# A second layer rewritten: step width first, tanh gate on half differences, fewer activation tables, fills on POOL

## The reference

```python
u = einsum('bld,hd->blh', x, W_x) + b_x                  # 256 hidden channels
g = sigmoid(einsum('bld,hd->blh', x, W_g) + b_g)
h = conv1d(u, conv_w, three taps, one filter per channel) + conv_b
u = u * g + h * (1.0 - g)
dt = clip(softplus(einsum('bld,hd->blh', x, W_dt) + b_dt).mean(axis=(0, 1)), 0.001, 2.0)
A_d = exp(-softplus(A_raw) * dt[:, None])                # 16 states per channel
B_d = (A_d - 1.0) / (A + 1e-06) * B_ssm
new = A_d * carry + B_d * u_t;  y_t = einsum('bhs,hs->bh', new, C_ssm)
attn = layernorm(x + y @ W_out.T + b_out)

gates = softmax(x @ gate_w);  top 2 of 8 experts, weight = sum of both gates
ffn = sum over chosen experts of weight * (gelu(x @ w1_e + b1_e) @ w2_e + b2_e)
```

## Time and profile before

| what | value |
| --- | --- |
| median of 3 runs | 433.61 us (428.1 to 437.87) |
| the profiled execution | 432.72 us |
| its span, first to last instruction | 430.9 us |
| mean granted TensorE clock | 0.951 |
| busy in the span: PE, DVE, ACT, POOL | 373.1, 305.1, 286.6, 168.6 us |

### The profile page before, as it was taken

How to read it: one execution, slowest core, us unless ns; L and a number is a source line. 1 busy time by engine, 2 the same in 40 slices (tenths; PEclk the granted TensorE clock), 3 DMA queues, 4 the chain that set the end, 5 groups by cost and what they waited for, 6 DMA issues and landing times. The chain is left out here.

```text
span 430.9 us, 10083 instructions
## 1 busy us (share of the span) xinstructions
PE 373.1 (87%) x3136; PEld 258.3 (60%) x3136; DVE 305.1 (71%) x1067; ACT 286.6 (67%) x689; POOL 168.6 (39%) x269
## 2 busy tenths in 40 slices
PE   1999999997999999999977999969788659788993
PEld 0444344366887777777764777766242435666982
DVE  4766709654988898989945588766989795384195
ACT  5787768564776776777736566556699942995634
POOL 1403909203787888888868022332000020000013
PEclk9999999999999999999999799989799678898997
DMA  8330323262222222222246100000000010000003
GB/s 227 65 87 12 100 79 105 70 177 68 56 72 70 72 73 73 75 73 73 85 125 152 20 2 2 0 2 0 2 0 1 0 27 2 0 2 0 2 0 99
DMA packets 33148, 23.14 MB, mean 54 GB/s; under 512 B 10062, under 2 KB 32860, under 8 KB 33116
## 3 DMA queue, kind: packets, MB, share of 16 engines
q1 hardware_dynamic: 31868, 22.67, 19.3%
q10 hardware_dynamic: 1248, 0.07, 0.2%
HBM read 13.26 MB, written 9.47 MB: 53 GB/s over the span
## 5 line engine op out<-in xcount | busy, mean ns | idle before, releaser
L486 PE MATMUL psum<-w,hT 128*128 128x385 f32 x128 | 45.5, 496 | 0.7 <-ACT stage L613 0.4
L900 PE MATMUL psum<-win,wst 128*32 128x128 f32 x1024 | 37.4, 277 | 1.3 <-ACT kd L975 1.3
L486 PEld LDWEIGHTS psum<-w,hT 128*128 128x128 f32 x128 | 23.2, 189 | 25.2 <-issue 11.4
L995 ACT ACTIVATE win<-psum 128x512 f32<-128x512 f32 x62 | 32.9, 581 | 0.1
L1266 ACT ACTIVATE std_<-mv_,cst 128x2 f32<-128x2 f32 (+1 forms) x46 | 13.5, 296 | 28.0 <-DVE mv_ L1244 16.4
L900 PEld LDWEIGHTS psum<-win,wst 128*32 128x32 f32 x1024 | 28.3, 109 | 5.5 <-ACT kd L975 1.5
L1004 ACT ACTIVATE bstd<-bmv,cst 128x1 f32<-128x1 f32 x32 | 9.4, 295 | 32.7 <-DVE bmv L1106 32.7
L1494 POOL TENSOR_TENSOR win<-win,lng 128x512 f32<-128x512 f32 x2 | 2.5, 1268 | 71.2 <-ACT win L1779 71.2
L1052 POOL TENSOR_SCALAR xh<-raw,bmv,brs 128x128 f32<-128x128 f32 x32 | 25.4, 793 | 2.7 <-DVE brs L1110 2.6
L1512 PE MATMUL psum<-xn1T,w1e 128*128 128x512 f32 x32 | 18.8, 714 | 7.7 <-ACT he L1673 6.1
L1045 POOL TENSOR_TENSOR xkm<-win,wst 128x256 f32<-128x256 f32 x32 | 19.6, 613 | 14.6 <-PE psum L918 8.4
(11 more groups left out here) (309 smaller groups left out, 1151.5 us busy)
## 6 DMA issues: line engine op xcount, KB each, us to landing
rows_scratch<-stage SPq DMA_DIRECT2D x32, 192.5 KB
win<-rows_scratch SPq DMA_DIRECT2D x32, 192.5 KB, 2.4
attn_scratch<-ob SPq DMA_DIRECT2D x32, 64.0 KB
att<-attn_scratch SPq DMA_DIRECT2D x4, 512.0 KB, 4.1
xt<-in_L_attn_x SPq DMA_DIRECT2D x4, 256.0 KB, 4.1
out<-win SPq DMA_DIRECT2D x4, 256.0 KB, 2.5
cst<-in_constants SPq DMA_DIRECT2D x1, 408.0 KB, 5.1
w<-in_L_attn_wk SPq DMA_DIRECT2D x2, 128.0 KB, 4.3
```

The source lines that it names most:

```text
L486: mm = nc.tensor.matmul(rows_bank(i, h)[:, 0:RC], hT[:, k, i * P:(i + 1) * P], w4[:, k, h, :], start=(k == 0), stop=(k == 1))
L900: mm = nc.tensor.matmul(dst[32 * b:32 * b + 32, 0:F], v[:, at:at + 2 * K], w_sb[:, state, first_slot(b) + h, :], start=False, stop=(h == 1 ...
L995: nc.scalar.activation(own, psum[:, 2 * half:2 * half + 2, 0:H * F].rearrange("p b (h g) -> p b h g", h=H), ACT.Copy).then_inc(w_done, 1)
```

## The change

- The step width's sum is split: softplus(x) = (|x| + x)/2 + ln(1 + exp(-|x|)). The sum of x needs no tile: the copies of the normalized input (`xn1T`) at the end of layer 0 sum up their columns (`accum_out` into `xsum`), and two 16-column products with W_dt follow the logits. Relu goes; Abs sums instead. Exp runs in two halves.
- The gate is 1 - g = (1 + tanh(-z/2))/2. The convolution's weights are halved and u is taken out of its middle tap once (`halve`), so that `conv` gives (h - u)/2, `blend` multiplies it by (gate + 1), and POOL adds u. `conv` writes in place in `uT`, on DVE alone; u has eight buffers.
- PE takes the dt products first and the gate products late, one with each expert tile; `pick` does one tile at a time.
- `decay()` runs after the third blend. ACT loads six tables in the block, not eleven.
- POOL clears `wtap` in four pieces, early, and copies `d0` and half of `wtap`, which ACT did.

```diff
+                m1.halve(nc, pool)
...
-                            ins = nc.scalar.activation(xn1T[:, i * P:(i + 1) * P], bank[6 + p][:, 0:P], ACT.Copy)
+                            ins = nc.scalar.activation(xn1T[:, i * P:(i + 1) * P], bank[6 + p][:, 0:P], ACT.Copy,
+                                                       accum_out=m1.xsum[:, i:i + 1])
                         ins.then_inc(cp_done, 1)
...
+        nc.gpsimd.tensor_scalar(self.cw[:, :, 1], self.cw[:, :, 1], 1.0, None, ALU.subtract).then_inc(self.halved, 1)
+        pool.wait_ge(self.halved, 1)
+        nc.gpsimd.tensor_scalar(self.cw[:], self.cw[:], 0.5, None, ALU.mult).then_inc(self.halved, 1)
+        nc.gpsimd.tensor_scalar(self.cb[:], self.cb[:], 0.5, None, ALU.mult).then_inc(self.halved, 1)
+        nc.gpsimd.tensor_scalar(self.bg[:], self.bg[:], -0.5, None, ALU.mult).then_inc(self.halved, 1)
...
-        gate = region1[:, :].rearrange("p (n l) -> p n l", n=NU)
+        gate = sb("gate", [P, RING, L], c=c)
...
+        region2 = sb("region2", [P, NG * P], c=c)
+        wtap = region2[:, :].rearrange("p (j c) -> p j c", j=NG)
+        gt = region2[:, 0:NT * P].rearrange("p (i q e) -> p i q e", i=NT, q=4)
+        ub = sb("ub", [P, NU, L + 2], c=c)
...
+        ab = region4[:, :].rearrange("p (n l) -> p n l", n=NU)
...
+        pick_bank = lambda n: bank[6 + n % 2]
...
+                def pick(n):
+                    t, q = divmod(n, 4)
+                    two = slice(32 * q, 32 * q + 2)
                     pe.wait_ge(gT_done, 4)
+                    if n >= 2:
+                        pe.wait_ge(gated, n - 1)
+                    nc.tensor.matmul(pick_bank(n)[:, :], con("pick")[two, :], gT[two, t * 512:t * 512 + 512],
+                                     start=True, stop=True).then_inc(pick_mm, 1)
...
+                dt_product(0)
+                for i in range(NT):
+                    nc.tensor.matmul(bank[7][:, i * NE:(i + 1) * NE], xn1T[:, i * P:(i + 1) * P], m1.gate_w[:], start=True, stop=True)
+                for k in range(2):
+                    mm = nc.tensor.matmul(bank[7][:, NT * (NE + k):NT * (NE + k + 1)], wT[:, 2, half(k)], m1.xsum[:], start=True, stop=True)
+                mm.then_inc(gate_mm, 1)
+                dt_product(1)
+                u_product(0)
+                dt_product(2)
+                dt_product(3)
+                for n in range(1, 5):
+                    u_product(n)
+                    dt_product(3 + n)
+                u_product(5)
+                gate_product(0)
+                gate_product(1)
+                pe.wait_ge(gates_done, 1)
+                turn_gates(0)
+                turn_gates(1)
+                u_product(6)
+                u_product(7)
+                up(0, 0)
+                up(0, 1)
+                for i in (2, 3):
+                    pe.wait_ge(gT_done, i - 1)
+                    turn_gates(i)
...
+                    pick(n)
+                    if n + 2 < NU:
+                        up(*divmod(n + 2, 4))
+                        gate_product(n + 2)
                     if n == 5:
+                        down(0)
+                for q in range(4):
+                    up(2, q)
+                    pick(8 + q)
+                    if q == 1:
+                        down(1)
...
+                    nc.scalar.activation(ub[:, n, 1:L + 1], bank[n % 2][:, :], ACT.Identity,
+                                         bias=m1.bx[:, n % 2:n % 2 + 1]).then_inc(u_done, 1)
+                def gate_tile(n):
+                    act.wait_ge(g_mm, n + 1)
+                    if n >= RING:
+                        act.wait_ge(blend_done, n - RING + 1)
+                    nc.scalar.activation(gate[:, n % RING, :], bank[2 + n % 2][:, :], ACT.Tanh,
+                                         bias=m1.bg[:, n % 2:n % 2 + 1], scale=-0.5).then_inc(gate_done, 1)
+                def magnitude(n):
+                    b, k = divmod(n, 2)
+                    act.wait_ge(dt_mm, n + 1)
+                    nc.scalar.activation(ab[:, n, :], bank[4 + n % 2][:, :], ACT.Abs, bias=m1.bd[:, k:k + 1],
+                                         accum_out=dta[:, k, b:b + 1]).then_inc(abs_done, 1)
+                def decayed(i):
+                    act.wait_ge(abs_done, NU // 2 * (i + 1))
+                    tiles = slice(NU // 2 * i, NU // 2 * (i + 1))
+                    nc.scalar.activation(ab[:, tiles, :], ab[:, tiles, :], ACT.Exp, scale=-1.0).then_inc(exp_done, 1)
...
+                act.wait_ge(a_stage, 1)
+                nc.scalar.activation(asp[:], asp[:], ACT.Exp, scale=-1.0).then_inc(a_stage, 1)
+                act.wait_ge(pads, 2)
+                magnitude(0)
+                magnitude(1)
                 u_tile(0)
+                act.wait_ge(mx_done, 1)
+                nc.scalar.activation(ex, lg, ACT.Exp).then_inc(ex_done, 1)
+                magnitude(2)
+                magnitude(3)
                 u_tile(1)
...
+                decayed(0)
+                for n in range(2, 6):
+                    magnitude(2 + n)
+                    u_tile(n)
+                decayed(1)
...
+                u_tile(6)
+                u_tile(7)
...
+                act.wait_ge(gates_done, 1)
+                for n in range(NU):
+                    hidden(*divmod(n, 4))
+                    gate_tile(n)
...
+                act.wait_ge(lnac_done, 1)
+                nc.scalar.activation(a32[:], lnac[:], ACT.Exp, scale=float(TC)).then_inc(a32_done, 1)
...
+                act.wait_ge(ex2_stage, 1)
+                nc.scalar.activation(ex2[:], ex2[:], ACT.Exp).then_inc(ex2_stage, 1)
...
-                nc.scalar.activation(d0[:, :, :, 1:NCH], a32[:, :, None, None].broadcast_to([P, NG, B, NCH - 1]), ACT.Copy).then_inc(d0_done, 1)
+                for q in range(4):
+                    hidden(2, q)
...
+                act.wait_ge(pool_stage, 5)
+                for q in range(2):
+                    nc.scalar.activation(wtap[quad(q), :, quad(q)], x2[quad(q), :, :].rearrange("p c j -> p j c"),
+                                         ACT.Copy).then_inc(taps, 1)
...
+                    b, k = divmod(n, 2)
+                    dst = uT[:, k, row(b)]
+                    dve.wait_ge(u_done, n + 1)
+                    nc.vector.tensor_scalar(dst, ub[:, n, 0:L], cw[:, k, 0:1], cb[:, k:k + 1], ALU.mult, ALU.add).then_inc(conv_done, 1)
+                    for tap in (1, 2):
+                        dve.wait_ge(conv_done, 3 * n + tap)
+                        nc.vector.scalar_tensor_tensor(out=dst, in0=ub[:, n, tap:L + tap], scalar=cw[:, k, tap:tap + 1],
+                                                       in1=dst, op0=ALU.mult, op1=ALU.add).then_inc(conv_done, 1)
...
+                    dve.wait_ge(conv_done, 3 * n + 3)
                     dve.wait_ge(gate_done, n + 1)
-                    nc.vector.tensor_tensor(df[:, p, :], df[:, p, :], gate[:, n, :], ALU.mult).then_inc(diff_done, 1)
-                    dve.wait_ge(diff_done, 2 * n + 2)
+                    nc.vector.scalar_tensor_tensor(out=dst, in0=gate[:, n % RING, :], scalar=1.0, in1=dst,
+                                                   op0=ALU.add, op1=ALU.mult).then_inc(blend_done, 1)
...
+                def decay():
+                    dve.wait_ge(abs_done, NU)
+                    w(nc.vector.tensor_reduce(dts[:], dta[:], AX, ALU.add))
+                    w(nc.vector.tensor_tensor(dts[:], dts[:], dtw[:], ALU.add))
+                    dve.wait_ge(a_stage, 3)
+                    w(nc.vector.scalar_tensor_tensor(out=asp[:], in0=asp[:], scalar=-1.0, in1=bsp[:], op0=ALU.mult, op1=ALU.subtract))
+                    dve.wait_ge(ln_done, 2)
+                    w(nc.vector.scalar_tensor_tensor(out=dt[:], in0=dts[:], scalar=0.5, in1=dtl[:], op0=ALU.mult, op1=ALU.add))
+                    w(nc.vector.tensor_scalar(dt[:], dt[:], 1.0 / TOK, 0.001, ALU.mult, ALU.max))
+                    w(nc.vector.tensor_scalar(dt[:], dt[:], 2.0, None, ALU.min))
+                    nc.vector.tensor_tensor(lna[:], asp[:], dt[:, :, None].broadcast_to([P, 2, NS]), ALU.mult).then_inc(lna_done, 1)
+                    dve.wait_ge(lna_done, 1)
+                    nc.vector.transpose(lnac[:], lna[:].rearrange("p k s -> p (k s)")).then_inc(lnac_done, 1)
+                    for k in range(2):
+                        nc.vector.tensor_tensor(kex[:, k, :, :], lna[:, k, None, :].broadcast_to([P, TC, NS]),
+                                                con("ramp0")[:, :, None].broadcast_to([P, TC, NS]), ALU.mult).then_inc(kex_stage, 1)
+                    dve.wait_ge(lnac_done, 1)
+                    nc.vector.tensor_tensor(ex2[:], lnac[:, :, None].broadcast_to([P, NG, TC]),
+                                            con("ramp1")[:, None, :].broadcast_to([P, NG, TC]), ALU.mult).then_inc(ex2_stage, 1)
+                    w(nc.vector.tensor_scalar(asp[:], asp[:], 1e-6, None, ALU.add))
...
+                gate_logits()
...
```

(37 more changed lines are left out.)

229 lines of the change are left out of this document (41 added, 188 removed).

## The result

The changed kernel takes a median of 442.66 us (439.06 to 443.83, four runs); the kernel before, beside it on the same chip, 432.47 (428.1 to 437.87). The ratio is 1.0222, with an interval of 1.0162 to 1.0281: about two per cent slower, where the forecast was 430.5 and no measurable change. The profiled execution of the changed kernel took 439.06 (span 437.3, mean granted clock 0.941), 6.3 above that of before.

The account below looks back on a forecast made before the run. The second layer's block was taken as a chain passing between engines, none full, with d0 the last wait before the first scan. -5.5 + 1.0 + 1.5 = -3.0 us gave 429.7, or 430.5 on the median's scale; range 424.5 to 439.

Parts of the forecast that it names:

- the step of 3.2: Among the blends before the transposes: one step charged 3.2 us because down(0) stands on PE ahead of pick(6).
- Blends (C): Blend steps from 325.0 to 349.6 us, 24.6 together, with DVE charged 0.92 or 0.65 per POOL add.
- The three steps of 1.9: Among the blends, after the third step that carries decay(): three steps charged 1.9 us each.
- the forecast's 1.0: Behind the scans: the last two picks wait for apply_gate(12) and (13), chunk_out behind them; 0.5 to 1.3, taken as 1.0 late.
- the first rival: POOL's adds don't hold DVE: blend steps lose about 0.65 to 1.0 each, time 425 (421 to 426); chance 0.20.
- d0 was the last wait: Before the first scan: ACT's fill of d0, to 378.49, is the last wait; taking it off ACT is worth 2.0 us.
- the second rival: POOL's copies of d0 and wtap run at the add's rate: 436, or 441 to 443 with transposes held; chance 0.19.
- The third rival: PE at the lower clock level through 325 to 350, among the blends: about 10 us more, 440; chance 0.09.
- the running sums: Ahead of the block: sixteen copies of xn1T each get a running sum; 0.8 to 3.2 us, taken as 1.5.
- B: Convolution, before the first blend: five convs 9.8 us, four gate-row copies 2.6, DVE waiting 3.8 for PE; ends at 325.0.

Follow-up runs that it names:

- e9: The changed kernel with picks 2 to 5 not made, their tiles multiplied by what earlier picks left; median 436.56 us, ratio 1.0074 to before.
- e2: The changed kernel without POOL's eight adds of u to the blended tiles; median 437.4 us, ratio 1.0120 to before.
- e7: The changed kernel with apply_gate(12) and (13) behind the sixth and seventh scan instead of the eighth; median 439.81 us, ratio 1.0060 to before.
- e3: The changed kernel with down(0) behind pick(7) on PE and add_experts(0) between the two transposes on DVE; median 437.47 us, ratio 1.0138 to before.
- e1: The changed kernel with picks 0 to 11 issued two at a time; median 435.73 us, ratio 1.0054 to before.
- e12: e11 with the picks one by one again, as in the changed kernel; median 424.03 us, ratio 0.9787 to before.
- e5: The changed kernel with 26 extra matmuls nobody reads, put where PE waits, to keep it busy; median 439.38 us, ratio 1.0143 to before.
- e11: e8 with apply_gate also ahead of conv and decay, as in e10; median 426.76 us, ratio 0.9873 to before.
- e10: The changed kernel with apply_gate(n) right behind blend(n), ahead of conv(n+6) and decay(); median 435.09 us, ratio 1.0080 to before.
- e4: The kernel before with only a32's Exp put behind t1's on ACT and d0 filled on POOL; median 437.43 us, ratio 1.0138 to before.
- e6: The changed kernel with all four copies of wtap on ACT and none on POOL; median 443.07 us, ratio 1.0210 to before.
- e8: The changed kernel with paired picks, down(0) late, add_experts(0) between transposes, wtap on ACT, apply_gates (8) to (13) earlier; median 424.58 us, ratio 0.9777 to before.

## Why the prediction was wrong

| step (changed kernel's time) | forecast | measured |
| --- | --- | --- |
| start of the block, later by | 1.5 | 0.53 |
| end of gates() | 309.6 | 310.41 |
| first blend | 325.5 | 325.95 |
| first blend to fourth | 13.8 | 13.59 |
| third apply_gate to seventh | 8.9 | 13.26 |
| start of the transposes | 350.7 | 354.60 |
| end of the fourth apply_gate behind them | 366.0 | 372.52 |
| down(2) to the add | 5.9 | 7.66 |
| first scan | 373.5 | 382.30 |
| behind the scan, later by | 1.0 | 2.6 |

(The forecast's times are given with the measured 0.53 of the block's start.)

**The step that failed is the step of 3.2 in the part "Blends (C)", "because down(0) stands on PE ahead of pick(6)": it took 7.43.** The three steps of 1.9 before it took 1.21, 1.90 and 2.72 from apply_gate to apply_gate, 5.83 for 5.7, and DVE waited for PE in the last of them alone (0.93). But PE fell behind meanwhile, and down(0) then stood in DVE's way almost whole. The prediction gives a single pick no price. e9's expectation names 0.27, about a quarter of the 1.14 of four, and a pick alone is 1.12. Between the third and the seventh apply_gate PE makes pick(4), two products, pick(5), two products, down(0) and pick(6); at full level, with the third apply_gate itself, that is 12.42 (e2, e7), against 8.9. Three picks at 0.85 more are 2.5 of the difference; the other 1.0 is down(0), which I let overlap with DVE's steps by more than PE's list allows. The lower level adds 0.8 in this execution. This split is arithmetic from rows. e3 shows that the step is down(0)'s: without it there, a2 to a6 is 8.8 and not 13.3, so 4.4 of its 4.56 lay in DVE's way, where the forecast charged 1.3 (3.2 less 1.9). No run shows that the picks' price alone, taken away, would come back as time; in e1, e9 and e12 it did not.

**Behind the transposes the lower level of PE cost what no term held.** The forecast had 15.3 from the transposes' start to the end of the fourth apply_gate behind them, and it was 17.9. Picks 10 and 11 wait for single apply_gates, with an `up` between them, in front of down(2). PE waited 3.85, and then the three took 2.0 to 2.1 each, 6.0 together; DVE's last apply_gate waited 1.82 for them, so the hold of ex2 ahead of it wasn't last. At the full level in e5 the three took 3.2, DVE didn't wait, and the stretch, less the 4.03 that add_experts(1) waited there, was 16.1; with the `up` ahead in e1 it was 16.0. So of the 2.6 some 0.7 would be there from ex2 alone, held for 1.4 where 0.6 was charged, and 1.9 are these three at the lower level.

**down(2) and the tail were mis-sized.** The forecast took 5.9 for down(2), near the row of before; the granted clock was 0.50 from 366 to 378, and it took 7.66: 1.8 more (4.8 at the full level in e11). Behind the scan picks 14 and 15 took 2.64 and the start of chunk_out ran at the lower level: 1.6 beyond the forecast's 1.0. In e1, e2, e3, e5 and e10, with the same lists there, the excess over before is 1.3 (50.0), inside the forecast's 0.5 to 1.3; so about 1.4 of the 1.6 is the level in this execution.

**What held.** gates() and the first blend came within 0.8 us of the forecast. POOL's adds hold DVE as charged (13.59 against 13.8; 11.1 without them), so the first rival was wrong. d0 was the last wait, worth 1.7 where the forecast said 2.0, and POOL's broadcasting copy took 3.50 as forecast. Of the second rival one part came true: wtap's two copies took 2.14 each, not the 1.04 of the rate in the earlier trace rows, and held ex2. The third rival was right that PE at the lower level is to be feared, but its place was behind the transposes more than in C. What the running sums cost can't be told: the block started 0.53 later, not 1.5, but e4, which has no running sums, started 0.72 later, and other kernels with them 0.4 (e5) to 3.8 later (e10). Two sums of the text are short of their own terms, by about 0.3 in B (16.2 from 309.1 give 325.3) and by 0.1 from C to down(2); neither matters here.

The terms add up: +3.9 to the transposes, +2.6 and +2.2 to the scan (the 1.8 of down(2), and 0.4 between the add and the scan), +1.6 behind it and -1.0 ahead of the block make 9.3 beyond the forecast's -3.0, so +6.3; the profiled execution is 6.34 above that of before. The medians differ by 10.2. That other executions are longer is seen in e6, whose list is the same up to the transposes: there down(1) ran at the lower level too, and the scan came 3.6 later. Of the 9.3 the lower level is 0.8 + 1.9 + 1.8 + 1.4, about 5.9, as read from rows; no run takes it away everywhere. In the changed kernel PE had waited ahead of each of these stretches. But a wait just ahead is not the whole of it: in e7 PE was busy without a gap from 339.06 on, with a granted clock of 1.00 to 352.5, and of 0.50 in the ten us behind, where down(1) stands; e5 and e6 fell at the same products. What decides in which place of an execution the level falls stays open.

## What to carry to other kernels

Before a burst's time is divided by its count, look whether its members ran one after the other: if the group's busy time is well under count times mean, they overlapped, and one alone costs the whole. When a chain hands tiles between two engines, lay out both lists with real lengths, and put long work that nobody awaits (here down(0)) behind the short product that somebody does. Work taken from an engine that isn't last pays only when the one that is last gets less; here ACT was relieved, PE's picks took 13 us more, and the same change with PE's and DVE's lists in another order and wtap on ACT is 1.7 to 2.8 per cent faster than the kernel before (e8).

## What the runs showed of the hardware

- Picks contract over two rows each, at four different places of the 128. One takes 1.12 us, two 1.13, four 1.14; at the lower level one takes 2.07 and four 2.09. The Trainium skill, "TensorE: Matmul & The Clock Gate", section "Why this matters for your kernels", says that products of few rows that lie in distinct row groups run at the same time, while a single one takes as long as one of all rows. This case's trace agrees: one pick is as long as an `up` (1.12 and 1.13).
- A copy on POOL held a one-input operation of DVE on 32 elements for 3.47 us (e4), and an add on POOL one on two elements for 1.08, while transposes beside d0's copy kept their length.
- POOL's copy of 32 x 1024 elements in another order took 2.14 us, 2.1 ns an element of a partition, against 0.88 ns for d0's 3968. ACT took 1.94 for the same copy.
- From 330 to 342 PE was busy for 12.00 of 12.00 us and had a granted clock of 0.68; ahead of it PE had waited 2.09 for ACT at 323.21.
